# The last layer of a four-layer transformer kernel: routing moved into the decay stage, one expert put inside each pair of heads, the experts' sum kept in a buffer

## The chip, the cores and the metric

The kernel runs on one core of one Trainium2 chip. The time is the device time of one launch in microseconds, as the median of three runs. The engines are TensorE (PE; its weight loads are listed as PEld), VectorE (DVE), ScalarE (ACT), GpSimd (POOL) and SyncE (SP), which only issues transfers. Each executes its own list of instructions in order, and semaphores connect them.

## The reference

The input x has 2 batches of 1024 tokens, 256 wide (T = 2048 tokens). There are four layers. In each, x is normalised and an attention part and a feed-forward part, both fed with the same normalised xn, are added to x. Only the last layer is touched.

```python
xn = _layernorm(x, axis=-1)
x = x + _L3_attn_ref(xn, ...) + _L3_ffn_ref(xn, ...)

# attention part: 32 heads, P = N = 64
zxbca = xn @ W_in.T                       # split into x_t, z_t, b_t, c_t, a_log
decay = exp(-exp(a_log))                  # one number per token and head
states = states * decay + x_t b_t         # a scan over the tokens
y = (states . c_t + x_t * D) * silu(z_t)
y = layernorm(y) * gamma + beta ;  return y @ W_out.T

# feed-forward part: 32 experts, 32 further columns without an expert, K = 8
scores = softmax(xn @ w_cls.T) ;  topk_idx = top_k(scores + bias, 8)
w = scores[topk_idx] / sum * 1.5
buf[e, pos] = xn of the tokens of expert e, at most CAP = 128 of them
y = (silu(g) * u) @ w_down[e],  g, u = split(buf[e] @ w_gate_up[e])
out = sum over k of w * y, times (1 + sum of w without an expert)
```

Since both parts read xn and only xn, the feed-forward part doesn't depend on the attention part of its layer.

## The kernel before, in words

x is kept transposed in SBUF as XT (128 partitions by 2 by 2048), its normalised form as XN beside it. A layer is a sequence of stages. Each stage is a block in which every engine gets its list of instructions; between blocks all engines meet. Products of float32 accuracy for the projections are made of three fp32r products: an operand is split into a rounded part (hi) and the rest (lo), and `split_product` (L199) adds hi*hi, hi*lo and lo*hi, over two halves of the 256 rows, so six passes of 512 columns for each bank. Matmuls of float32 take two passes.

The last layer has these stages:

1. The norm, n3.
2. `l3_decays`: the decays of all heads (L1965 to L1989), stored to DRAM as running products and as themselves; the bias column bcol from beta (L1970), and the output weights wout scaled by gamma on DVE (L1995).
3. For each batch: `split_stage` of XN into XH and XL; `l3_pairs`; `l3_output`, which normalises Y, multiplies by wout and adds to XT (L2330).
4. `moe_route` (L2399 to L2523): the logits (L2428), the softmax and the top 8 on DVE, for each expert a running number of each of its tokens (`place`, L2439), the table of token numbers and weights `info`, and `key`. XN and XT are transposed to rows of tokens (L2436) and stored to DRAM: XN as moe_xtok, XT as the first content of the kernel's output.
5. `moe_experts`: for each of 32 experts a one-hot matrix of 128 slots by 2048 tokens (DVE, L2658), a product with `info` that gives the token number and weight of each slot (`mx_ptab`, L2609), the index (DVE, L2666 to L2672), a gather of 128 rows (POOL, L2587), two transposes (L2621), gate and up (L2628), silu (ACT, L2647), the product with up (DVE, L2684), down (L2635), the weight (ACT, L2650), and a scatter that adds the rows to the output in DRAM (POOL, L2597). Indices, gathered rows and weights are double-buffered or better.

`l3_pairs` runs over 16 pairs of heads, and in each over two halves z of the batch's tokens (512 each). The first pair is written out, the other 15 are a loop. The order in the half (h, z) is:

- TensorE: project x, b, c, z into four banks (L199), the outputs of the half before (L2097, L2102), the transposes of x (L2110) and b (L2114), the scores (L2121), the sums for the states pds (L2128), which need btok and xtok.
- ACT: copies xT, bT, cT; silu of z to sz; with z = 1 the hi part of the next pair's weights (L2145); xtok (L2167).
- DVE: two scans that build the decay table (L2221), cdT (L2224), the skip term of the half before (L2212, into the tile skip), btok (L2232), mixT (L2235), dsm (L2239), three or four updates of the state (L2246, L2250).
- POOL: with z = 1 the lo part of the next weights (L2189); for the half before, Y = skip * sz (L2179, "the gate") and ysum += Y (L2185).
- SP: the pair's weights (w4), the decays as table input (decb) and as rows (prow), and D (dcol).

The tiles xtok, mixT, sz, xT, cdT have two buffers, and the banks px, pb, pc, pz, pds, py one each; psc takes two.

Of the kernel before, what the change touches and what calls it, by code (L numbers as in the profile page):

```python
# [7 lines left out]
F32 = mybir.dt.float32  # L8
# [8 lines left out]
P = 128  # L17
# [146 lines left out]
def split_stage(nc, name, src, hi, lo):  # L164
# [4 lines left out]
    with Stage(nc, name) as st:  # L169
# [3 lines left out]
        with nc.Block() as block:  # L173
# [13 lines left out]
            @block.gpsimd  # L187
            def _(pool):
                for i, (c, tok) in enumerate(parts):
                    if i % 3 == 2:  # L190
                        pool.wait_ge(rounded, i + 1)
                        pool.tensor_tensor(lo[:, c, tok], src[:, c, tok], hi[:, c, tok].bitcast(F32), ALU.subtract)

# [1710 lines left out]
def l3_attn(nc, k, a):  # L1904

    decays = nc.dram_tensor("l3_decays", [2, L3_HEADS, T], F32, kind="Internal").ap()
    with Stage(nc, "l3w") as sw:
        wout = sw.sb("wout", [P, L3_PAIRS, D])  # L1910
        bcol = sw.sb("bcol", [P, DC])
        l3_decays(nc, k, a, decays, wout, bcol)
        for b in range(B):
            l3_batch(nc, k, a, decays, b, wout, bcol)


def l3_batch(nc, k, a, decays, b, wout, bcol):
    with Stage(nc, f"l3a{b}") as st:
        Y = st.sb("Y", [P, L3_PAIRS, S])
        ysum = st.sb("ysum", [P, S])  # L1920
        with Stage(nc, f"l3x{b}") as sx:
            XH, XL = sx.sb("XH", [P, DC, S], F32R), sx.sb("XL", [P, DC, S], F32R)
            split_stage(nc, f"l3s{b}", k.XN[:, :, b * S:(b + 1) * S], XH, XL)
            l3_pairs(nc, k, a, decays, b, Y, ysum, XH, XL)
# [5 lines left out]
def l3_decays(nc, k, a, decays, wout, bcol):  # L1930


    with Stage(nc, "l3d") as st:
# [6 lines left out]
        acc = [st.ps(f"acc{i}") for i in range(2)]  # L1940
        loaded, made, exped, decayed, prods, stored = st.sem("loaded"), st.sem("made"), st.sem("exped"), st.sem("decayed"), st.sem("prods"), st.sem("stored")
        zeroed = st.sem("zeroed")
        gb = st.sb("gb", [P, 2, L3_PAIRS])
        pbeta = st.ps("pbeta")
        w_loaded, beta_made = st.sem("w_loaded"), st.sem("beta_made")
        with nc.Block() as block:

            @block.sync
            def _(sp):
                sp.dma_start(w[:, :, :], rows(a["L3_wa"])).then_inc(loaded, 16)  # L1950
                sp.dma_start(gb[:, :, :], a["L3_gb"]).then_inc(w_loaded, 16)
                sp.dma_start(wout[:, :, :], rows(a["L3_W_outT"])).then_inc(w_loaded, 16)
                sp.wait_ge(prods, NCH)
# [3 lines left out]
                sp.wait_ge(stored, 32)  # L1957

            @block.tensor
            def _(pe):  # L1960
                pe.wait_ge(loaded, 16)
                for j in range(NJ):
                    wait(pe, exped, j - 1)
                    for c in range(DC):
                        mm = pe.matmul(acc[j % 2][0:H, :], w[:, c, :], k.XN[:, c, j * BANK:(j + 1) * BANK], start=(c == 0), stop=(c == DC - 1))  # L1965
                    mm.then_inc(made, 1)
# [4 lines left out]
                mm.then_inc(beta_made, 1)  # L1971

            @block.scalar
            def _(act):
                for j in range(NJ):
                    act.wait_ge(made, j + 1)
                    act.activation(ex[:, j % 2, :], acc[j % 2][0:H, :], ACT.Exp).then_inc(exped, 1)
                    act.wait_ge(exped, j + 1)
                    act.activation(dec[:, j * BANK:(j + 1) * BANK], ex[:, j % 2, :], ACT.Exp, scale=-1.0).then_inc(decayed, 1)

            @block.vector
            def _(dve):
                dve.memset(zero[:, :], 0.0).then_inc(zeroed, 1)
                dve.wait_ge(zeroed, 1)
# [7 lines left out]
                dve.wait_ge(beta_made, 1)  # L1992
                dve.tensor_copy(bcol[:, :], pbeta[:, 0:DC])
                for i in range(L3_PAIRS):
                    dve.tensor_scalar(wout[:, i, :], wout[:, i, :], gb[:, 0, i:i + 1], None, ALU.mult)  # L1995


def l3_pairs(nc, k, a, decays, b, Y, ysum, XH, XL):


    with Stage(nc, f"l3p{b}") as st:
# [11 lines left out]
        xtok = st.sb("xtok", [P, 2, QUAD, P])  # L2013
        btok = st.sb("btok", [P, QUAD, P])
        table = st.sb("table", [P, 2, BANK])
        mixT = st.sb("mixT", [P, 2, 2, BANK])
        dsm = st.sb("dsm", [P, QUAD, P])
        state = st.sb("state", [P, 2, QUAD, P])
        skip = st.sb("skip", [P, BANK])
# [790 lines left out]
```

## Time and profile before

| | us |
|---|---|
| median of three runs | 3949.11 (3946.87 to 3950.89) |
| span of the profiled execution | 3953.8 |
| PE busy in it | 3518.6 (89%) |
| DVE busy | 2363.0 (60%) |
| ACT busy | 1546.2 (39%) |
| POOL busy | 1385.1 (35%) |

The span goes from the first to the last instruction of the profiled execution, and it is the only time given for that execution; the median of the unprofiled runs is 4.7 us below it. A busy share is a mean over all stages. The page of the profile cuts the span in 40 slices of about 99 us; the last layer fills the last twelve of them.

### The profile page before, as it was taken

Reading aid. Unit: us, or ns where it says so; the run is one execution under the profiler, and the core shown is the slowest. Engines: PE = TensorE matmul, PEld = TensorE weight load, DVE = VectorE, ACT = ScalarE, POOL = GpSimd, SP = SyncE. Lnnn points to the kernel's source line nnn. Section 1 sums busy time; section 2 is a strip of 40 time slices with the busy share of each in tenths; the row PEclk is TensorE's granted clock in tenths of the full one; section 3 lists DMA queues with packets and bytes.
Section 4 is the critical chain, followed back from the end, with each engine's and each line's share of the span. In section 5 each row is a group of like instructions: output and inputs, shape, how many; then the busy total and the mean of one; then the engine's idle time right before and its main releaser. Section 6 shows DMA issues by size and latency. Waiting matters only on the chain. (4 is left out here: it accounts for less than half of the span.)

```text
span 3953.8 us, 65993 instructions
## 1 busy us (share of the span) xinstructions
PE 3518.6 (89%) x21608; PEld 2645.3 (67%) x21608; DVE 2363.0 (60%) x4783; ACT 1546.2 (39%) x2820; POOL 1385.1 (35%) x1085
## 2 busy tenths in 40 slices
PE   6899999999796999999995779998699988999576
PEld 4777777777574888888872445554388847886354
DVE  3555555655423566666654879885477756776454
ACT  2444444444333444444432236664333333333121
POOL 1333333332133666666652200000133352335144
PEclk8999999999898999999997879999799998999755
DMA  0000000000001000000000412221233304331144
GB/s 33 7 5 3 5 5 3 5 5 5 33 0 43 13 18 17 17 17 17 17 5 22 171 65 82 80 83 39 65 93 103 105 10 107 98 96 48 60 108 96
DMA packets 115990, 178.66 MB, mean 45 GB/s; under 512 B 22288, under 2 KB 65040, under 8 KB 115600
## 3 DMA queue, kind: packets, MB, share of 16 engines
q1 hardware_dynamic: 109776, 169.38, 13.7%
q0 software_dynamic: 6144, 8.39, 1.3%
q8 instruction: 38, 0.62, 0.1%
q14 instruction: 32, 0.26, 0.0%
HBM read 151.51 MB, written 25.95 MB: 45 GB/s over the span
## 5 line engine op out<-in xcount | busy, mean ns | idle before, releaser
L424 POOL TENSOR_TENSOR l0h_probs<-l0h_probs,l0h_inv 128x128 f32<-128x128 f32 (+7 forms) x256 | 292.7, 1146 | 585.4 <-DVE l0h_inv L459 585.4
L1775 DVE TENSOR_REDUCE l2h_half<-l2h_s 128x1 f32<-128x512 f32 x512 | 337.3, 685 | 48.0 <-PE l2h_s L1677 47.0
L355 PE MATMUL l0h_sc<-l0a_KT,l0h_QT 128*128 x768 | 296.7, 499 | 29.8 <-ACT l0h_probs L528 28.3
L1762 ACT ACTIVATE l2h_PT<-l2h_s 128x1024 f32<-128x1024 f32 x256 | 248.3, 1022 | 162.6 <-PE l2h_s L1687 162.5
L382 PE MATMUL l0h_cx<-l0h_PT,l0h_VG 128*128 128x128 f32 x2304 | 300.7, 276 | 0.0
L528 ACT ACTIVATE l0h_probs<-l0h_sc,l0h_negtop 128x128 f32<-128x128 f32 (+7 forms) x256 | 189.6, 741 | 245.0 <-DVE l0h_negtop L454 244.6
L382 PEld LDWEIGHTS l0h_cx<-l0h_PT,l0h_VG 128*128 128x128 f32 x2304 | 278.0, 192 | 1.1
L159 POOL TENSOR_TENSOR XN<-XN,n_rstd 128x512 f32<-128x512 f32 x32 | 39.8, 1266 | 595.8 <-DVE n_rstd L140 595.8
L1677 PE MATMUL l2h_s<-l2h_K,l2h_Q 128*128 128x512 f32 x512 | 218.5, 466 | 23.2 <-DMA l2h_K<-l_split 21.0
L452 DVE TENSOR_REDUCE l0h_top<-l0h_sc 128x1 f32<-128x128 f32 (+7 forms) x256 | 193.9, 758 | 8.8
L355 PEld LDWEIGHTS l0h_sc<-l0a_KT,l0h_QT 128*128 128x128 f32 x768 | 125.7, 192 | 106.3 <-issue 63.6
L391 PE MATMUL l0h_outp<-l0h_ctxT,l0h_wd 128*128 128x128 f32 x1024 | 163.8, 283 | 24.8 <-ACT l0h_ctxT L521 11.7
L369 PEld LDWEIGHTS l0h_tp<-ident,l0h_probs 128*128 128x128 f32 x1152 | 138.6, 141 | 64.1 <-issue 39.5
L1677 PEld LDWEIGHTS l2h_s<-l2h_K,l2h_Q 128*128 128x128 f32 x512 | 99.2, 195 | 113.4 <-DVE l2h_half L1775 74.7
L369 PE MATMUL l0h_tp<-ident,l0h_probs 128*128 128x128 f32 x1152 | 168.7, 273 | 0.0
L470 DVE COPY l0h_PT<-l0h_tp 128x256 f32<-128x256 f32 (+2 forms) x192 | 98.6, 514 | 114.2 <-PE l0h_tp L369 112.4
L2189 POOL TENSOR_TENSOR l3p_w_lo<-l3p_w,l3p_w_hi 128x1024 fp32r<-128x1024 f32 x34 | 80.1, 2356 | 241.1 <-ACT l3p_w_hi L2145 241.1
L391 PEld LDWEIGHTS l0h_outp<-l0h_ctxT,l0h_wd 128*128 128x128 f32 x1024 | 134.2, 191 | 44.7 <-ACT l0h_ctxT L521 31.2
L514 ACT ACTIVATE l0h_PT<-l0h_tp 128x512 f32<-128x512 f32 (+1 forms) x192 | 100.8, 525 | 159.8 <-PE l0h_tp L369 159.3
L2221 DVE TENSOR_TENSOR_SCAN l3p_table<-l3p_decb,l3p_eye 128x512 f32<-128x512 f32 x128 | 149.6, 1210 | 22.8 <-DMA l3p_blk<-c_l_block 17.3
L1687 PE MATMUL l2h_s<-l2h_Q,l2h_K 128*128 128x512 f32 x512 | 161.7, 399 | 0.0
L2179 POOL TENSOR_TENSOR l3a_Y<-l3p_skip,l3p_sz 128x512 f32 (+1 forms) x64 | 81.6, 1276 | 208.9 <-DVE l3p_skip L2212 208.9
(408 smaller groups left out, 8954.9 us busy)
## 6 DMA issues: line engine op xcount, KB each, us to landing
l3p_decb<-l_decays SPq DMA_DIRECT2D x128, 256.0 KB, 4.2
l3p_w<-L_w SPq DMA_DIRECT2D x34, 512.0 KB, 3.7
l2h_Q<-l_split SPq DMA_DIRECT2D x64, 256.0 KB
l2h_K<-l_split SPq DMA_DIRECT2D x64, 256.0 KB
l3p_prow<-l_decays SPq DMA_DIRECT2D x128, 128.0 KB, 2.9
l_split<-l2q_hi SPq DMA_DIRECT2D x16, 512.0 KB, 4.1
l_split<-l2q_lo SPq DMA_DIRECT2D x16, 512.0 KB, 3.8
mx_wgu<-L_ffn_w_gate_up SPq DMA_DIRECT2D x32, 256.0 KB
```

What stands on the lines that cost most here:

```text
L355: mm = pe.matmul(sc[u % 2][:, lo:lo + n], QT[:, u * P:(u + 1) * P], KT[:, ds(g, 1), b * S + lo:b * S + lo + n], start=True, stop=True)
L369: mm = pe.transpose(tp[n % 2][:, (kb - q) * P:(kb - q + 1) * P], probs[:, u % 4, kb * P:(kb + 1) * P], k.ident[:, :])
L382: mm = pe.matmul(cx[:, 0:P], VG[:, b * NQ + kb, :], PT[:, u % 2, kb, :], start=(kb == 0), stop=(kb == t))
L391: mm = pe.matmul(outp[:, c * P:(c + 1) * P], wd[:, c * P:(c + 1) * P], ctxT[:, u % 2, :], start=True, stop=True)
L424: pool.tensor_tensor(p, p, inv[:, u % 4:u % 4 + 1].to_broadcast([P, keys(u)]), ALU.mult).then_inc(probs_scaled, 1)
L452: dve.reduce_max(top[:, u % 2:u % 2 + 1], sc[u % 2][:, 0:keys(u)], AX_X).then_inc(top_ready, 1)
L528: act.activation(probs[:, u % 4, 0:keys(u)], sc[u % 2][:, 0:keys(u)], ACT.Exp, bias=negtop[:, u % 2:u % 2 + 1], scale=L0_SCALE, accum_out= ...
L1677: pe.matmul(bank(slot_of(i))[:, :], Q1[:, b, t * P:(t + 1) * P], K1[:, b, z * BANK:(z + 1) * BANK], start=True, stop=True).then_inc(s1_mad ...
L1687: mm = pe.matmul(s2[kb % 2][:, z * BANK:(z + 1) * BANK], K2[:, b, kb * P:(kb + 1) * P], Q2[:, b, z * BANK:(z + 1) * BANK], start=True, sto ...
L1762: act.activation(PT[:, b, kb, :], s2[kb % 2][:, :], ACT.Exp, scale=L2_SCALE).then_inc(exped, 1)
L1775: dve.reduce_max(half[:, b, t, z:z + 1], bank(slot_of(i))[:, :], AX_X).then_inc(s1_read, 1)
L2221: dve.tensor_tensor_scan(table[:, i, :], decb[:, o, i, :], eye4[:, :], 0.0, ALU.mult, ALU.add).then_inc(tables, 1)
```

## The change

Layer 3 becomes one function, `l3_layer`, with these stages:

- `l3_front` takes the place of `l3_decays` and `moe_route`. It holds the decays, the routing, the table, and the rows of XN. The rows of XT and their store to the output are gone. A zeroed tile is stored to a new DRAM buffer, moe_acc. The scaling of wout and the copy of bcol are ACT's.
- `split_in_place`: only XH has a tile of its own. XL is written over XN, through a second name (XNL) for the same memory. All its subtractions are DVE's.
- `l3_pairs` carries expert 16 b + h inside pair h of batch b. The loop is now over pairs 1 to 14; pairs 0 and 15 are written out.
- `l3_finish` loads moe_acc, transposes XT to rows, adds, and stores the output in four parts and a last row of tiles.

Two PSUM banks were needed: pds now shares the bank of pz, and the freed bank pm holds gathered rows or the down product in its left half, table or gate and up in its right one. To make room in SBUF, xtok and mixT have one buffer, and skip is gone: DVE writes to Y and POOL multiplies Y in place. The experts' tiles have one buffer each.

The core of the diff, the front:

```diff
+def l3_front(nc, k, a, decays, wout, bcol, moe):
             @block.sync
-                sp.dma_start(w[:, :, :], rows(a["L3_wa"])).then_inc(loaded, 16)
+                sp.dma_start(w[:, :, :], rows(a["L3_wa"])).then_inc(wa_loaded, 16)
+                sp.dma_start(wcls[:, :, :], rows(a["L3_ffn_w_clsT"])).then_inc(loaded, 16)
...
+                sp.wait_ge(zero_rows, 2)
+                sp.dma_start(rows(acc), rowsZ[:, :, :]).then_inc(stored, 16)
...
+                sp.wait_ge(tr_act, turns)
+                sp.dma_start(rows(xtok), rowsN[:, :, :]).then_inc(stored, 16)
             @block.tensor
...  (decay products as before)
+                pe.wait_ge(loaded, 80)
+                for t in range(TT):
+                    for c in range(DC):
+                        mm = pe.matmul(lg[:, t * MOE_N:(t + 1) * MOE_N], k.XN[:, c, t * P:(t + 1) * P], wcls[:, c, :], ...)
+                mm.then_inc(logits_made, 1)
+                for n in range(turns):   # the transposes of XN
...
                 pe.wait_ge(w_loaded, 32)   # pbeta
...
+                pe.wait_ge(counted, 1)     # place
             @block.vector
...  (decay scans as before, then the routing of moe_route, unchanged)
```

Inside the pairs, TensorE and DVE:

```diff
                 def step(h, z):
-                    project(h, z)
+                    project(h, z, (0, 1))
+                    if z == NZ - 1:
+                        gate_up(h)
+                    project(h, z, (2, 3))
                     if not is_first(h, z):
                         outputs(*before(h, z))
-                    tables_and_states(h, z)
+                    if z == 0:
+                        turn_rows(h)
+                    else:
+                        down(h)
+                    scores(h, z)
+                    if z == NZ - 1 and more(h):
+                        table(h + 1)
+                    state_sums(h, z)      # now also waits for z_kept
+                table(0)
                 steps(pe, step)
@@ DVE, in step(h, z), after cdT
+                    if z == NZ - 1:
+                        gate_expert(h)
+                    if more(h):
+                        mark(h + 1, z)    # one half of the one-hot
                     if not is_first(h, z):
                         add_skip(*before(h, z))
@@ after mixT, which now waits for y_made of the half before
+                    if z == 0:
+                        keep_index(h)
+                    elif more(h):
+                        make_index(h + 1)
                     dve.wait_ge(ds_made, n + 1)
@@ ahead of the steps
+                dve.wait_ge(e_consts, 32)
+                mark(0, 0)
+                mark(0, 1)
+                make_index(0)
+                def keep_index(e):
+                    dve.wait_ge(indexed, e + 1)
+                    wait(dve, scattered, 16 * e)
+                    dve.tensor_copy(index_out[:, :], index_in[:, :]).then_inc(kept_index, 1)
+                    wait(dve, weighed, e)
+                    dve.tensor_copy(wcol[:, :], idw[:, 1:2]).then_inc(kept_index, 1)
```

POOL, ACT and SP:

```diff
@@ POOL
                 def step(h, z):
                     if z == NZ - 1:
                         split_weights(h + 1)
+                        if more(h):
+                            gather(h + 1)
                     if not is_first(h, z):
                         gate(*before(h, z))
+                    if z == NZ - 1:
+                        scatter(h)
@@ ACT, z == 1: after cT
+                        act.activation(gated[:, :], pm[:, D:D + P], ACT.Silu).then_inc(sg_kept, 1)
@@ ACT, z == 1: after the split of the next weights
+                        act.wait_ge(down_made, h + 1)
+                        act.wait_ge(kept_index, 2 * h + 2)
+                        wait(act, scattered, 16 * h)
+                        act.activation(ye[:, :], pm[:, XR], ACT.Copy, scale=wcol[:, 0:1]).then_inc(weighed, 1)
@@ ACT, z == 0: after xtok
+                        act.activation(xgT[:, :], pm[:, XR], ACT.Copy).then_inc(xg_kept, 1)
@@ SP, in load(h, z), between decb and prow
+                    if z == NZ - 1:
+                        wait(sp, gu_made, h)
+                        sp.dma_start(wgu[:, :, :], a["L3_ffn_w_gate_up"][ds(E0 + h, 1)]...).then_inc(e_loaded, 16)
+                        wait(sp, down_made, h)
+                        sp.dma_start(wdn[:, :], a["L3_ffn_w_down"][ds(E0 + h, 1)]...).then_inc(e_loaded, 16)
@@ SP, ahead of load(0, 0)
+                sp.dma_start(slots[:, :], a["c_moe_slots"].to_broadcast([P, P])).then_inc(e_consts, 16)
+                sp.dma_start(spare[:, :], a["c_moe_spare"]).then_inc(e_consts, 16)
```

The last stage:

```diff
+def l3_finish(nc, k, a, acc):
+                sp.dma_start(summed[:, :, :], rows(acc)).then_inc(loaded, 16)
+                for i in range(PARTS):      # 4
+                    t = slice(i * TT // PARTS, (i + 1) * TT // PARTS)
+                    sp.wait_ge(added, (i + 1) * N // PARTS)      # N = 8
+                    sp.dma_start(rows(a["out"])[:, t, :], out_rows[:, t, :]).then_inc(stored, 16)
...
+                for n in range(N):          # TensorE
+                    wait(pe, added, n - 3)
+                    ... four transposes of XT into tr[n % 4]
+                for n in range(N):          # DVE
+                    dve.wait_ge(turned, n + 1)
+                    dve.tensor_tensor(out_rows[:, t, :], summed[:, t, :], tr[n % 4][:, :]..., ALU.add).then_inc(added, 1)
```

## Rows read from the trace of the kernel before

**Rows 1.** Busy time by stretch, with granted clock (PEclk), DMA share and GB/s.

```profile
3539.97:3560.96 20.99, 20.99 (x161) 17.88 (x160) 15.56 (x22) 6.92 (x11) 7.45 (x6) 1.00 0.35 100
...
3745.00:3950.00 205.00, 141.56 (x896) 102.23 (x896) 97.44 (x160) 37.34 (x97) 96.47 (x64) 0.50 0.45 102
```

**Rows 2.** Timeline, stage borders: start us, us, engine, line, operation, idle and releaser.

```profile
3690.51 0.75 DVE L2330 SCALAR_TENSOR_TENSOR XT<-l3o_tmp,l3w_bcol,XT 128x512 f32<-128x512 f32 x1
...
3692.22 0.40 SPq L2405 DMA_DIRECT2D mr_wcls<-L_ffn_w_clsT  x1
...
3740.95 0.69 DVE L2523 SCALAR_TENSOR_TENSOR moe_key<-mr_maskE,mr_place 128x512 f32<-128x512 f32 x1
...
3943.78 1.57 POOL L2597 DMA_INDIRECT out<-mx_y,mx_index  x1 [4.42 <-ACT mx_y L2650]
```

**Rows 3.** DMA issues (KB, us to landing), and transposes in the timeline.

```profile
l3w_wout<-L_W_outT SPq DMA_DIRECT2D x1, 2048.0 KB, 8.5
...
out<-mr_rowsX SPq DMA_DIRECT2D x1, 2176.0 KB, 10.6
...
3712.10 3.62 PE L2436 MATMUL mr_tr<-ident,XN 128*128 128x128 f32 x16
```

**Rows 4.** DMA issues of POOL in the experts: count, us to landing.

```profile
mx_xg<-moe_xtok,mx_index POOLq DMA_INDIRECT x32, 2.7
...
out<-mx_y,mx_index POOLq DMA_INDIRECT x32, 4.0
```

**Rows 5.** Decays and logits: busy time in two windows, then the timeline.

```profile
2822.00:2826.00 4.00, 4.00 (x30) 3.62 (x28) 2.79 (x9) 1.24 (x3) 0.00 (x0) 0.87 0.00 0
...
3698.00:3712.00 14.00, 13.61 (x64) 13.61 (x65) 1.62 (x2) 0.00 (x0) 0.00 (x0) 0.50 0.00 1
...
2822.39 11.51 PE L1970 MATMUL l3d_pbeta<-l3d_gb,l3w_wout 128*128 128x1 f32 x64
...
2834.01 4.28 DVE L1995 TENSOR_SCALAR l3w_wout<-l3w_wout,l3d_gb 128x256 f32<-128x256 f32 x16
...
3698.39 13.91 PE L2428 MATMUL mr_lg<-mr_wcls,XN 128*128 128x64 f32 x64 [14.14 <-DMA mr_again<-c_moe_again]
...
3712.34 1.23 DVE L2463 TENSOR_REDUCE mr_small<-mr_lg 128x16 f32<-128x1024 f32 x1 [10.85 <-PE mr_lg L2428]
```

**Rows 6.** Timeline of single experts: TensorE, DVE.

```profile
3758.97 0.61 PE L2609 MATMUL mx_ptab<-moe_info,mx_onehot 128*128 128x7 bf16 x16
...
3759.87 1.22 PE L2635 MATMUL mx_py<-mx_wdn,mx_gated 128*128 128x256 f32 x2 [0.28 <-DVE mx_gated L2684]
...
3912.65 0.17 DVE L2666 TENSOR_REDUCE mx_idw<-mx_ptab 128x2 f32<-128x6 f32 x1
...
3913.10 0.16 DVE L2672 TENSOR_TENSOR mx_index<-mx_spill,mx_idw 128x1 uint32<-128x1 f32 x1
...
3913.25 2.29 DVE L2658 TENSOR_TENSOR mx_onehot<-mx_slots,moe_key 128x2048 bf16<-128x2048 f32 x1
```

**Rows 7.** Timeline: first instructions of the pairs, and one half (z = 0).

```profile
2849.59 0.80 PE L199 MATMUL l3p_px<-l3x_XH,l3p_w_hi 128*128 128x512 f32 x1 [15.70 <-POOL l3p_w_lo L2189]
...
2850.76 2.34 DVE L2221 TENSOR_TENSOR_SCAN l3p_table<-l3p_decb,l3p_eye 128x512 f32<-128x512 f32 x2 [8.56 <-DMA l3p_blk<-c_l_block]
...
3550.37 0.47 PE L199 MATMUL l3p_px<-l3x_XH,l3p_w_hi 128*128 128x512 f32 x1
...
3560.05 1.16 PE L2128 MATMUL l3p_pds<-l3p_xtok,l3p_btok 128*128 128x128 f32 x8
```

**Rows 8.** Timeline of DVE and POOL in the same pair.

```profile
3541.29 1.12 DVE L2250 SCALAR_TENSOR_TENSOR l3p_state<-l3p_state,l3p_prow,l3p_dsm 128x128 f32<-128x128 f32 x3
...
3551.18 1.29 POOL L2185 TENSOR_TENSOR l3a_ysum<-l3a_ysum,l3a_Y 128x512 f32<-128x512 f32 x1 [0.21 <-POOL l3a_Y L2179]
...
3551.43 1.97 DVE L2250 SCALAR_TENSOR_TENSOR l3p_state<-l3p_state,l3p_prow,l3p_dsm 128x128 f32<-128x128 f32 x3
...
3559.12 0.69 DVE L2232 TENSOR_TENSOR l3p_btok<-l3p_pb,l3p_table 128x512 f32<-128x512 f32 x1 [0.23 <-PE l3p_pb L2114]
```

More of the change, by code:

```diff
@@ L1927, in l3_batch @@
         clear_semaphores(nc)
-def l3_decays(nc, k, a, decays, wout, bcol):
-    with Stage(nc, "l3d") as st:
+def l3_front(nc, k, a, decays, wout, bcol, moe):
+    key, info, xtok, acc = moe.key, moe.info, moe.xtok, moe.acc
+    with Stage(nc, "l3f") as st:
         H = L3_HEADS
@@ L1991, in _, with per_tile @@
                 dve.memset(dec[:, :].rearrange("h (i n) -> h i n", n=P)[:, :, 0:1], 0.0).then_inc(zeroed, 1)
[L1992 to L1998, printed above, removed]
+                def per_tile(i):
+                    return small[:, i, :].unsqueeze(2).to_broadcast([P, TT, MOE_N])
@@ L2001, in l3_pairs @@
+def l3_pairs(nc, k, a, decays, b, Y, ysum, XH, XL, moe):
+    E0 = b * L3_PAIRS
+    key, info, xrows, acc = moe.key, moe.info, moe.xtok, moe.acc
     with Stage(nc, f"l3p{b}") as st:
@@ L2033, in steps, with more @@
                 step(0, z)
-            with engine.Fori(1, L3_PAIRS) as h:
+            with engine.Fori(1, L3_PAIRS - 1) as h:
                 for z in range(NZ):
                     step(h, z)
+            for z in range(NZ):
+                step(L3_PAIRS - 1, z)
+        def more(h):
+            return not isinstance(h, int) or h + 1 < L3_PAIRS
         def before(h, z):
@@ L2129, in tables_and_states, with table, turn_rows @@
                     mm.then_inc(ds_made, 1)
+                def table(e):
+                    pe.wait_ge(marked, 2 * e + 2)
+                    wait(pe, weighed, e)
+                    for t in range(TT):
+                        mm = pe.matmul(pm[:, TAB], onehot[:, t, :], info[:, ds(E0 + e, 1), t, :].rearrange("p a n -> p (a n)"), start=(t == 0), stop=(t == TT - 1))
+                    mm.then_inc(tabled, 1)
+                def turn_rows(e):
+                    pe.wait_ge(gathered, 16 * e + 16)
+                    pe.wait_ge(indexed, e + 1)
+                    for c in range(DC):
+                        mm = pe.transpose(pm[:, c * P:(c + 1) * P], xg[:, c * P:(c + 1) * P], k.ident[:, :])
+                    mm.then_inc(g_turned, 1)
@@ L2731 @@
 SPLIT_LAYERS = (0, 1)
[L2732 removed]
+LAYERS = [(l0_attn, l0_ffn), (l1_attn, l1_ffn), (l2_attn, l2_ffn)]
 def program(nc, a):
```

583 lines of the change are left out of this document (269 added, 314 removed).

## The prediction

> **What bounds the kernel now.** I read the busy shares by stage first. Within one pair of heads TensorE is busy for the whole of its 20.99 us at full clock, DVE 74%, ACT 33%, POOL 35%; in the experts it is busy 69% at half clock and waits in between [rows 1]. So the pairs are TensorE's, and whatever is put into them costs its TensorE time and no more, as long as nothing it waits for is late. The experts are a chain of short steps and transfers with nobody saturated. The timeline gives the stage borders: the attention's last instruction ends at 3691.3 us (3690.51 + 0.75), the routing's last at 3741.6, and the last scatter is issued at 3943.8 in a span of 3953.8 [rows 2]. Routing and experts together hold 3953.8 - 3691.3 = 262.5 us at the end, which the change dissolves.
>
> **1. What is removed, and the last stage.** 262.5 us go. In their place: 1.0 us to enter a stage (3691.3 to the routing's first load at 3692.2), the load of acc, the additions, the stores. A 2,048 KB load took 8.5 us to landing, the 2,176 KB store to out 10.6 [rows 3]. Four transposes take 0.9 us at half clock [rows 3]; the first four groups lie under the load, the others are chained to the additions (0.7 us each), so the last addition ends about 5.2 us behind the landing. The stores start 1.6 us behind it and need 10.6, which ends later. Behind a landing comes what the old end shows: 10.0 us from the issue of the last scatter to the end of the span, less its 4.0 us to landing [rows 2, 4], so 6.0. Sum: 1.0 + 8.5 + 1.6 + 10.6 + 6.0 = 27.7; as the chain by the additions gives only 25, I take 27 (bounds 22 and 34). Net: **-235.5**.
>
> **2. The front stage.** The order written for TensorE puts the logits behind the decay products, so the routing starts only at 2822.4 [rows 5], and its five loads, issued behind one other on SP's queue, have landed by then: at the old place the logits could start 6.2 us behind the first of them (3698.4 against 3692.2), which here is 2817.5 [rows 2, 5]. The logits took 13.9 us, all at half clock; DVE's chain from their end (3712.3) to the key (3741.6) is 29.3 us [rows 5]. Now the logits follow matmuls that ended at full clock: the mean of 2822 to 2826 is 0.87, so some 3 us more at full clock [rows 5]. Those halve: I take 11.0 us (bounds 7.0, all fast, and 13.9). The stage ends at 2822.4 + 11.0 + 29.3 = 2862.7 instead of 2838.3 (2834.01 + 4.28) [rows 5]: **+24.5** (20.5 to 27.5). Under this chain at no cost: transposes of XN, pbeta (11.5 us on TensorE, over at about 2853), the product for place, the zeros and both large stores (POOL and the DMA engines are idle), and the scaling of wout, which moves to ACT (16 from about 2853 on; ACT's mean in a pair, 6.92 us for 11 mostly twice as wide [rows 1], puts their end at 2863 at the latest). That cover is the thinnest: what ACT takes beyond it lengthens the stage one for one.
>
> **3. The start of the pairs, twice.** TensorE began at 2849.6, DVE at 2850.8, when its constants had landed [rows 7]. Now two more DMAs stand ahead of them on SP (+0.8), DVE makes both halves of the one-hot (2.29 us for a whole one [rows 6]) and TensorE's queue begins with table(0) (0.6), which waits for them. 1.2 + 0.8 + 2.4 + 0.6 = 5.0, twice: **+10** (8 to 13). The splitting's fourth subtraction goes from POOL to DVE; ACT's rounding sets its end as before: 0.
>
> **4. Inside the pairs, 32 times: TensorE.** A pair takes 20.99 us [rows 1]. Added are 8 passes of gate and up; eight such 128x128 passes took 0.91 us in the pairs (3560.05 to the border at 3560.96) [rows 1, 7]. The down product: 1.22 us for two passes at half clock, 0.43 at full without its tail; two transposes 0.25 (sixteen took 3.62 at half clock [rows 3]); 16 table products 0.61 at half clock, of which a floor of issue may stay: 0.4 [rows 6]. Sum **2.0** (1.8 to 2.3, with a bubble at each of four waits).
>
> **5. Inside the pairs: who may be late.** Per pair DVE gets 2 x 1.2 (mark), 0.3, 0.6 (index, from the reduction to the last of three) and 0.3, so 3.6 on its 15.6 of now 23; ACT 1.1; POOL 1.0 to 2.4 for a gather and 1.6 for a scatter [rows 6, 4]. None is full. I follow one pair, time 0 being the start of its second half (z = 1) at TensorE. Gate and up stand at 2.9, DVE's product for them is done at 7.2, down stands at 8.1: hidden. ACT's w_hi still ends before 8.2, POOL's w_lo by 10.8, the next pair starts at 12.0. The table is at 10.8 to 11.2; DVE makes the index behind mixT, by 12.8, so 0.8 into the next pair. POOL's gather is queued there, ahead of the gate of the first half: issued at 1.0, landed at 3.8 (2.7 to landing [rows 4]), wanted by turn_rows at 7.6: 3.8 us spare. SP's two weight loads wait for the previous expert's products; behind them stands prow, which waits longer, for the states at 3.4 of the next pair, so they hold back nothing. The scatter goes out near 6 and lands near 10; DVE's keep_index asks for it at 11, and what is queued behind that (dsm, the states) has over 3 us until TensorE's outputs.
>
> The narrow place is btok. In the first half it ended 0.24 us before TensorE's product of it started (3559.12 + 0.69 against 3560.05, 9.7 us into the pair) [rows 7, 8]. The transposes of the gathered rows give 0.25 more, and make_index pushes DVE's dsm back by 0.4, which the wait for y_made absorbs only if mark (1.2) is over by then. And the gate on POOL, held back by the gather, now falls beside DVE's state updates and scans. A row shows what that costs: three updates took 1.12 us alone, but 1.97 where POOL's ysum of 1.29 began 0.25 before them [rows 8].
>
> The Trainium skill (SBUF — State Buffer, Who interferes with whom) states it as a rule: a Vector instruction with two SBUF inputs and a GpSimd instruction that reads SBUF exclude each other, the first to start keeping the port for its whole length. By that rule the scans and mark, too, stand back behind POOL, which no row here shows for them; by rule alone the time would be that of rival B.
>
> Without a collision btok ends at 9.7, wanted at 9.9: stall 0. If POOL's first pass stands in a scan's way and the second in mark's way, I get btok at 10.25 and the product at 10.5: stall 0.6. If both passes precede a scan each: 1.3. I take **0.6**, a pair then costs 2.6, and 32 x 2.6 = **+83** (58 at 1.8 and no stall, 144 at 4.5, if scatter and gather should each hold DVE for another microsecond).
>
> **Sum.** -235.5 + 24.5 + 10 + 83.2 = -117.8: the span of 3953.8 becomes 3836.0. The median of the runs, 3949.1, is 4.7 under the profiled span; I keep that distance: **3831 us**.
>
> **Rivals.** A, no collision: DVE keeps its slack and a pair costs TensorE's 2.0 alone: 19 us less, **3812**. For it: its 23 us hold only 19 of DVE; against: POOL's gate now starts just where the states run. B, both POOL passes get ahead: 3.3 per pair, 22 more, **3854**. For it: the 1.97 row; against: the scans are issued back to back, so POOL has to win a tie.
> C, slower than before: the gathered rows come late. turn_rows stands in TensorE's in-order queue ahead of the scores of both heads, so each microsecond of delay past the 3.8 spare is one of stall, 32 times. It decides from 118 / 32 = 3.7 us of stall, when a gather takes 2.8 + 3.8 + 3.7 = 10.3 us from issue to landing. If it took 12, the stall is 5.4 and the time 3831 + 173 = **4004**, and a lower granted clock after such gaps would come on top. For it: gather and scatter share POOL's one queue with the gate, and decay rows are read at a DMA share of 0.35; against: with the experts' share of 0.45 it landed in 2.7 [rows 1, 4].
> D, the change does only half of what it says: the front is serial, the decays hiding nothing. That is already in the 24.5.
> [...]
>
> **How the numbers follow.** Forecast 0.45 (own range 3818 to 3845), A 0.2, B 0.2, C 0.05; 0.1 remains for a front, start or end outside its bounds by tens of microseconds. The range takes in A and B with their bounds, 3798 to 3880. All but C and a part of the last are faster by over 0.2% (8 us, what this kernel's measurement can tell from nothing): faster 0.92, same 0.02, slower 0.06.
>
> **What would show it.** Right: a pair of 23 to 24 us, TensorE still full and at full clock there; a front stage of 52 us, its logits partly fast; 27 us behind the attention; first projection 5 us later than before in each batch. The stall of step 5 would be an idle of 0.3 to 1.3 us ahead of the product of btok in first halves alone, with POOL's gate over a scan. Wrong: TensorE waiting for the gather or for DVE's product of the expert, a granted clock under 0.95 in the pairs, or DVE busy through a whole pair.

## The result, and the profile after

The changed kernel takes 3836.7 us (median of four runs, 3834.8 to 3841.9) against 3949.2 us before on the same chip: a ratio of 0.971 (95% interval 0.970 to 0.972). The profiled execution has a span of 3840.0 us against 3953.8, 113.8 less; 117.8 less was predicted. By stage, from the timelines of both:

| part | before, us | after, us | difference | predicted |
|---|---|---|---|---|
| ahead of the front | 2810.8 | 2811.4 | +0.5 | 0 |
| front, to VectorE's last result | 27.5 | 48.3 | +20.9 | +24.5 |
| start of the pairs, both batches | 24.2 | 33.8 | +9.7 | +10 |
| pairs, to the output stage, both | 693.8 | 790.8 | +96.9 | +83.2 |
| output stages, both | 135.0 | 136.4 | +1.4 | 0 |
| behind the last output stage | 262.5 | 19.4 | -243.1 | -235.5 |

The front in the timeline of after (start, duration, engine, line, operation, operands; in brackets the idle time before and what ended it):

```profile
2811.35 0.37 SPq L2008 DMA_DIRECT2D l3f_w<-L_wa  x1
2822.92 7.36 PE L2042 MATMUL l3f_lg<-l3f_wcls,XN 128*128 128x64 f32 x64
2830.32 1.22 DVE L2099 TENSOR_REDUCE l3f_small<-l3f_lg 128x16 f32<-128x1024 f32 x1 [3.47 <-PE l3f_lg L2042]
2858.98 0.69 DVE L2159 SCALAR_TENSOR_TENSOR l3w_key<-l3f_maskE,l3f_place 128x512 f32<-128x512 f32 x1
```

The logits start at 2822.9, 0.5 us behind the 2822.4 of the prediction, and take 7.36 us where they took 13.9 [rows 5]. VectorE's chain behind them, from 2830.32 to 2859.67, is 29.3 us as read before. ScalarE's scaling of wout ended at 2856.5, inside it, so the thin cover held.

The start of the first batch of pairs:

```profile
2863.37 0.37 SPq L2259 DMA_DIRECT2D l3p_slots<-c_moe_slots  x1
2867.53 0.43 SPq L2263 DMA_DIRECT2D l3p_blk<-c_l_block  x1
2869.78 2.34 POOL L2443 TENSOR_TENSOR l3p_w_lo<-l3p_w,l3p_w_hi 128x1024 fp32r<-128x1024 f32 x1 [5.45 <-ACT l3p_w_hi L2386]
2873.48 2.36 DVE L2491 TENSOR_TENSOR l3p_onehot<-l3p_slots,l3w_key 128x1024 bf16<-128x1024 f32 x2 [10.37 <-DMA l3p_blk<-c_l_block]
2875.90 0.59 PE L2338 MATMUL l3p_pm<-l3w_info,l3p_onehot 128*128 128x7 bf16 x16 [22.65 <-DVE l3p_onehot L2491]
2876.34 0.77 PE L222 MATMUL l3p_px<-l3x_XH,l3p_w_hi 128*128 128x512 f32 x1
```

The weights are split at 2872.1, and nothing else that the first projection reads comes later. In TensorE's order it stands behind the table, which needs the marks (the one-hot), and these stand behind VectorE's wait for blk, a constant they don't use.

One pair, from the first projection product of its second half (z = 1) to that of the next pair's:

```profile
3656.18 0.48 PE L222 MATMUL l3p_px<-l3x_XH,l3p_w_hi 128*128 128x512 f32 x1
3659.02 1.05 PE L2353 MATMUL l3p_pm<-l3p_xgT,l3p_wgu 128*128 128x128 f32 x8
3664.47 0.70 PE L2359 MATMUL l3p_pm<-l3p_wdn,l3p_gated 128*128 128x256 f32 x2
3667.06 1.36 PE L2338 MATMUL l3p_pm<-l3w_info,l3p_onehot 128*128 x16
3669.26 0.48 PE L222 MATMUL l3p_px<-l3x_XH,l3p_w_hi 128*128 128x512 f32 x1
3680.29 0.48 PE L222 MATMUL l3p_px<-l3x_XH,l3p_w_hi 128*128 128x512 f32 x1
```

A window over exactly this stretch, with busy time and count of each engine, then the granted clock, the DMA share and GB/s:

```profile
3656.18:3680.29 24.11, 23.99 (x190) 20.41 (x188) 20.59 (x30) 7.73 (x14) 11.05 (x7) 1.00 0.50 114
```

The half z = 1 takes 13.08 us (10.40 before), the half z = 0 10.92 in the first batch and 11.03 in the second (10.6 before). TensorE (first number after the length) is busy for all but 0.1 us, at full clock. The table products (L2338) are the row out of line: 1.36 us for 16 products which took 0.59 at the start of the batch, shown above, and 0.61 at half clock before [rows 6]. From 3667.06 the next work of TensorE follows 1.31 us later.

Where the predicted collision would be (z = 0, VectorE and GpSimd):

```profile
3597.80 0.99 POOL L2449 DMA_INDIRECT l3p_xg<-moe_xtok,l3p_index_in  x1 [3.26 <-DVE l3p_index_in L2505]
3597.95 3.82 DVE L2567 SCALAR_TENSOR_TENSOR l3p_state<-l3p_state,l3p_prow,l3p_dsm 128x128 f32<-128x128 f32 x3
3598.82 1.30 POOL L2434 TENSOR_TENSOR l3a_Y<-l3a_Y,l3p_sz 128x512 f32 x1
3600.33 1.29 POOL L2439 TENSOR_TENSOR l3a_ysum<-l3a_ysum,l3a_Y 128x512 f32<-128x512 f32 x1 [0.20 <-POOL l3a_Y L2434]
3601.69 2.33 DVE L2529 TENSOR_TENSOR_SCAN l3p_table<-l3p_decb,l3p_eye 128x512 f32<-128x512 f32 x2
3601.78 2.54 POOL L2456 DMA_INDIRECT moe_acc<-l3p_ye,l3p_index_out  x1 [0.16 <-issue]
```

Three state products take 3.82 us, against 1.12 and 1.97 in [rows 8]. The scans behind them start when GpSimd's second pass has just ended, and keep their 1.17 us each.

The end of a batch of pairs, in the kernel before (first line) and after, and the last stage of after:

```profile
3196.47 0.17 DVE L2314 MEMSET l3o_avg<- 128x128 f32 x1 [3.21 <-PEq L2044]
...
3264.57 0.75 DVE L2485 SCALAR_TENSOR_TENSOR l3a_Y<-l3p_xT,l3p_dcol,l3p_py 128x512 f32<-128x512 f32 x1 [3.19 <-PE l3p_py L2302]
3266.86 1.26 POOL L2439 TENSOR_TENSOR l3a_ysum<-l3a_ysum,l3a_Y 128x512 f32<-128x512 f32 x1 [0.20 <-POOL l3a_Y L2434]
3271.17 0.17 DVE L2631 MEMSET l3o_avg<- 128x128 f32 x1 [5.85 <-PEq L2236]
...
3820.92 0.38 SPq L2690 DMA_DIRECT2D fin_summed<-moe_acc  x1
3829.57 4.29 DVE L2714 TENSOR_TENSOR fin_out_rows<-fin_summed,fin_tr 128x512 f32<-128x512 f32 x7 [8.93 <-DMA fin_summed<-moe_acc]
3830.88 4.23 SPq L2694 DMA_DIRECT2D out<-fin_out_rows  x4
3835.16 0.81 SPq L2695 DMA_DIRECT2D out<-fin_summed  x1
```

The idle time ahead of the output stage is 5.85 us; before it was 3.21. The last stage is a chain of load (8.6 us), eight additions (5.2) and a last store: 19.4 us.

### The profile page after: what moved, and what is told of

It is laid out like the page before. It is cut to its first block and busy times, and to the rows that moved or that the text cites. A ratio compares the mean times of both kernels' runs of the same rounds, so it can differ in the third digit from the quotient of the medians.

```text
span 3840.0 us, 66211 instructions
## 1 busy us (share of the span) xinstructions
PE 3466.9 (90%) x21608; PEld 2618.4 (68%) x21608; DVE 2420.7 (63%) x4872; ACT 1537.1 (40%) x2827; POOL 1403.2 (37%) x1083
## 5 line engine op out<-in xcount | busy, mean ns | idle before, releaser
L378 PE MATMUL l0h_sc<-l0a_KT,l0h_QT 128*128 x768 | 298.2, 501 | 29.2 <-ACT l0h_probs L551 27.5
L414 PE MATMUL l0h_outp<-l0h_ctxT,l0h_wd 128*128 128x128 f32 x1024 | 163.9, 283 | 24.5 <-ACT l0h_ctxT L544 11.7
L994 ACT ACTIVATE l1a_kswap<-l1a_pk,l1a_bias 64x512 f32<-64x512 f32 x64 | 43.8, 685 | 278.3 <-PE l1a_pk L222 278.3
```

The lines of the kernel that those rows point to most:

```text
L378: mm = pe.matmul(sc[u % 2][:, lo:lo + n], QT[:, u * P:(u + 1) * P], KT[:, ds(g, 1), b * S + lo:b * S + lo + n], start=True, stop=True)
L414: mm = pe.matmul(outp[:, c * P:(c + 1) * P], wd[:, c * P:(c + 1) * P], ctxT[:, u % 2, :], start=True, stop=True)
```

## The experiments

Each names what it changes in the kernel after. Their ratios are to the kernel before on the same chip.

### The table at a fixed expert

```diff
-  pe.matmul(pm[:, TAB], onehot[:, t, :], info[:, ds(E0 + e, 1), t, :]..., start=(t == 0), stop=(t == TT - 1))
+  pe.matmul(pm[:, TAB], onehot[:, t, :], info[:, E0:E0 + 1, t, :]..., start=(t == 0), stop=(t == TT - 1))
```

> The 16 table products of every pair read the token table at a fixed expert instead of at the loop's expert, so the experts' gate weights belong to the wrong expert (each row still gets one); all else is as in the changed kernel. Theory 1: the table costs 1.31 us in the loop's pairs against 0.42 to 0.56 in the written-out ones because each product's address comes from a loop register. Then the table falls to 0.4 to 0.6 us in every pair, the pair from 24.0 to about 23.1 us, and 28 or so loop pairs take 23 to 27 us off: about 3812 us (ratio to before 0.965). Rival: the table is slow because of what the other engines do to its operands beside it (or because its operand was written shortly before): then it stays at 1.3 us, the pair at 24.0 and the time at 3836.

Measured: 3818.5 us, ratio 0.967 (0.965 to 0.969). The 16 products of 12 pairs (2905 to 3200 us) grouped by line, in the kernel after and then here (count | busy us, mean ns | idle before):

```profile
L2338 PE MATMUL l3p_pm<-l3w_info,l3p_onehot 128*128 x192 | 16.2, 173 | 0.0
```

```profile
L2338 PE MATMUL l3p_pm<-l3w_info,l3p_onehot 128*128 128x7 bf16 x192 | 6.7, 167 | 0.0
```

Per pair that is 1.35 us and then 0.56. The mean of one hardly moves (173 and 167 ns): a product isn't slower, they follow each other at 82 ns on average instead of 26. The trace's records, register instructions included, have the reason: in the loop each of the 16 has one more instruction on TensorE's queue, which makes the operand's address from the loop's register, 448 of them in 28 loop pairs; in the written-out pairs and in this kernel there is none. With them the first eight products of a table start about 26 ns apart and the others 124; without them all do at about 26. The half z = 1 falls from 13.09 to 12.20 us. The gain, 18 us, is smaller than the expected 23 to 27 because z = 0 grew from 10.92 to 11.15 (11.03 to 11.26 in the second batch), which the next experiment shows as well.

The register address alone doesn't fix the price. The experts' loop of the kernel before had it too (384 such instructions for 24 experts), and there a table took 0.72 us on average (0.61 to 1.15), because 12 to 16 of its products started about 27 ns apart before the first gap of 124. The written-out experts took 0.59 to 0.61. Why more products come close together there was not tested.

### The expert's slice of the table, copied

```diff
+  def keep_info(e):
+      wait(act, tabled, e)
+      act.activation(einfo[:, :], info[:, ds(E0 + e, 1), :, :]..., ACT.Copy).then_inc(info_kept, 1)
@@ ACT, z == 0: after xgT:  keep_info(h + 1)
@@ PE, table(e):
+  pe.wait_ge(info_kept, e + 1)
-  ... info[:, ds(E0 + e, 1), t, :] ...
+  ... einfo[:, t * MOE_INFO:(t + 1) * MOE_INFO] ...
```

> ScalarE copies the expert's slice of the token table into a tile at a fixed address, once per pair in the half after xgT, and the table products read that tile; the full computation. Theory 1 (loop-register addresses): table 0.4 to 0.6 us, pair about 23.1, time 3810 to 3816 if ScalarE's copy (0.3 to 0.5 us more per pair, it is busy 40%) stays beside TensorE. Rival 1 (the table is slow for another reason): 3836. Rival 2 (the added copy delays ScalarE's xT copies, on which the scores wait): the pair loses up to 0.5 us in the half z = 0, so that 8 to 15 of the 25 us come back.

Measured: 3817.6 us, 0.967 (0.965 to 0.969); halves of 12.20 and 11.15 (11.26). The address theory stands with the whole computation in place: one register-addressed instruction on ScalarE instead of 16 on TensorE. Rival 2 has the right half, z = 0, which lost 0.23 us per pair, but the wrong reason. What z = 0 lost is TensorE's wait for btok, in all products of btok of 13 pairs:

```profile
L2333 PE MATMUL l3p_pz<-l3p_xtok,l3p_btok 128*128 128x128 f32 x208 | 29.8, 286 | 2.9 <-DVE l3p_btok L2554 2.9
```

2.9 / 13 = 0.22 us per pair by this row; by the halves it is 0.30 and 0.40, against the 10.85 us of the next experiment, where the wait is 0. The fixed-expert kernel, which has no copy on ScalarE, has the same 2.9, and in the kernel after this row read 1.1. One pair shows how GpSimd's two passes now fall:

```profile
3577.62 2.70 DVE L2577 SCALAR_TENSOR_TENSOR l3p_state<-l3p_state,l3p_prow,l3p_dsm 128x128 f32<-128x128 f32 x3
3580.25 3.37 DVE L2539 TENSOR_TENSOR_SCAN l3p_table<-l3p_decb,l3p_eye 128x512 f32<-128x512 f32 x2
3580.37 2.16 POOL L2449 TENSOR_TENSOR l3a_ysum<-l3a_ysum,l3a_Y 128x512 f32<-128x512 f32 x1 [0.20 <-POOL l3a_Y L2444]
```

The second pass began 0.12 us behind the first scan and took 2.16 us instead of 1.29; the second scan, behind that pass, took 2.24 instead of 1.21. So the scans are held here, in 30 of the 32 pairs, which in the kernel after happened in 2.

### The gating product ahead of the gather

```diff
@@ POOL, step(h, z)
   split_weights(h + 1)
-  if more(h): gather(h + 1)
   gate(*before(h, z))
+  if more(h): gather(h + 1)
   scatter(h)
```

> GpSimd does the gating product of the pair ahead of the gather instead of behind it; the full computation. The collision that the prediction priced at 0.6 us per pair was seen at 3.83 us for three state products on VectorE beside gather and gate, with the wait of the gather's turn-over at TensorE for the token column at 0.05 to 0.3 us. Theory: the stall in z = 0 is that collision; with the gate first the state products run 1.5 to 2.5 us and the 0.05 to 0.3 us of stall go, 2 to 8 us in all: 3829 to 3835. Rival: the gather, 1.3 us later, lands too late for its turn-over and its wait grows: the pair gets longer than 24.0 and the time is 3840 or more. Rival 2: the extra 0.05 in z = 0 isn't a stall by the collision: no change, 3836.

Measured: 3831.9 us (3831.7 to 3838.0), 0.971 (0.969 to 0.972), 4.8 less than after. The runs of both kernels overlap (3834.8 to 3841.9 there), so what follows rests on the halves in the traces. Timeline of z = 0, then the row of btok:

```profile
3592.73 1.27 POOL L2439 TENSOR_TENSOR l3a_ysum<-l3a_ysum,l3a_Y 128x512 f32<-128x512 f32 x1 [0.20 <-POOL l3a_Y L2434]
3594.67 1.13 DVE L2567 SCALAR_TENSOR_TENSOR l3p_state<-l3p_state,l3p_prow,l3p_dsm 128x128 f32<-128x128 f32 x3
3594.89 1.01 POOL L2449 DMA_INDIRECT l3p_xg<-moe_xtok,l3p_index_in  x1 [0.89 <-DVE l3p_index_in L2505]
...
L2331 PE MATMUL l3p_pz<-l3p_xtok,l3p_btok 128*128 128x128 f32 x200 | 28.6, 286 | 0.0
```

The states are back at 1.13 us although the gather's issue lies right beside them, so the two passes of the gate held them, not the gather. z = 0 becomes 10.85 us in both batches: the stall was 0.07 per pair in the first and 0.18 in the second, 30 x 0.12 = 3.8 us. The transposes of the gathered rows (the turn-over) aren't waited for, so the first rival falls. The slack shows too: between the states and btok VectorE now waits four times, 0.19, 0.46, 0.89 and 0.42 us, and in the kernel after not at all.

### No experts in the pairs

All expert work is out of the pairs (marks, index, table, gather, products, scatter and the loads of their weights), and the output lacks that layer's experts.

> The experts are taken out of the pairs: no marks, index, table, gather, turn-over, gate/up, down, scatter and no loads of their weights there (the output lacks the experts' contribution of this layer); the front and the finish stay. Theory: all of the pair's growth (20.99 to 24.0) is the expert's own TensorE work and stalls, and the pair falls back to 20.99 exactly, the gap between the last pair and the output stage from 5.9 back to 3.2 us of VectorE idle time and the start of a batch by about 5 us: 32 x 3.0 + 2 x 2.6 + 2 x 5 = 111 us less than 3836, about 3725. Rival: part of the growth is from the rearrangement (weight splits, gating and queue order around the experts' places): then the pair stays above 21.2 us and the time above 3732. Rival on the end gap: if it is not the last scatter's, it stays at 5.9 us.

Measured: 3733.4 us, 0.946 (0.944 to 0.947). From the first projection product of a batch to that of its last half are 326.3 and 327.2 us here, 326.2 and 325.9 before and 370.7 and 371.8 after: of the growth of 90.4, 1.4 is left without experts, so next to nothing is from the rearrangement. A pair before is 21.05 us on this measure. The start and the end of a batch:

```profile
2867.61 2.34 POOL L2416 TENSOR_TENSOR l3p_w_lo<-l3p_w,l3p_w_hi 128x1024 fp32r<-128x1024 f32 x1 [5.48 <-ACT l3p_w_hi L2372]
2870.00 0.80 PE L222 MATMUL l3p_px<-l3x_XH,l3p_w_hi 128*128 128x512 f32 x1 [18.70 <-POOL l3p_w_lo L2416]
...
3215.96 0.17 DVE L2587 MEMSET l3o_avg<- 128x128 f32 x1 [3.21 <-PEq L2236]
```

The projection starts with the split's end, and the end gap is 3.21 us: both went with the experts. The whole gain, 103 us, is 8 short of the 111 expected. By the traces (104.4 in all) the pairs with their end gaps gave 96.4 where 101 was taken (3.0 for each of 32 pairs, but the last halves hold no table), and the two starts 8.0 where 10 was.

### The marks ahead of the wait for the constants

```diff
@@ DVE
-  dve.wait_ge(consts, 32)
   mark(0, 0); mark(0, 1); make_index(0)
+  dve.wait_ge(consts, 32)
```

> VectorE's wait for the two constants of the scans (eye4 and blk) moves behind the first two marks and the first index; the full computation. Theory: what makes a batch of pairs start late is that the first marks stand behind a wait for constants they don't use (blk landed at 2873.48 while the weights' split, which the first projection waits for, ended at 2872.12): the marks run from about 2867, the table comes before the split's end and the first projection at 2872.1 instead of 2876.3, 4.2 us per batch, 8 in all: about 3828. Rival: the marks wait for the slots' load as long as for blk (it is the tail of DMA landing that counts): under 2 us per batch, time 3834 or more.

Measured: 3828.9 us, 0.970 (0.968 to 0.971), 7.7 less than after, as expected; in the traces the two starts of the pairs take 25.6 us together instead of 33.8.

```profile
2864.82 0.37 SPq L2259 DMA_DIRECT2D l3p_slots<-c_moe_slots  x1
2868.76 2.36 DVE L2489 TENSOR_TENSOR l3p_onehot<-l3p_slots,l3w_key 128x1024 bf16<-128x1024 f32 x2 [4.20 <-DMA l3p_spare<-c_moe_spare]
2871.18 0.59 PE L2338 MATMUL l3p_pm<-l3w_info,l3p_onehot 128*128 128x7 bf16 x16 [16.56 <-DVE l3p_onehot L2489]
2873.54 0.79 PE L222 MATMUL l3p_px<-l3x_XH,l3p_w_hi 128*128 128x512 f32 x1 [1.77 <-POOL l3p_w_lo L2443]
```

From the first load to the projection are 8.7 us instead of 13.0, and what the projection waits for is the split of its weights again.

### The product with beta ahead of the logits

```diff
@@ PE, l3 front
+  pe.wait_ge(w_loaded, 32);  64 products of wout with gb into pbeta
   pe.wait_ge(loaded, 80);    64 products of XN with wcls into lg
   the transposes of XN
-  pe.wait_ge(w_loaded, 32);  64 products of wout with gb into pbeta
```

> In the front the 64 one-column products of wout with beta go ahead of the 64 router products instead of behind them; the full computation. The logits were seen at 7.36 us right behind the decays' products at full clock, where the prediction took 11.0 and the kernel before showed 13.91 at the low clock. Theory 1 (the clock decides what the logits cost, and one-column work for 10 us lets it fall): pbeta takes 6.5 to 10.8 us, then the logits 11 to 13.9 instead of 7.36; the routing chain starts 12 to 17 us later and the front is as much longer: 3849 to 3854. Rival (the clock doesn't fall over pbeta, or the logits' time isn't the clock's): the logits stay at 7.4 us and the front grows by pbeta's 6.5 to 10.8 alone, less 0.2: 3843 to 3847.

Measured: 3862.7 us, 0.978 (0.976 to 0.979): 26 more than after, which neither theory had.

```profile
2826.37 13.81 PE L2042 MATMUL l3f_pbeta<-l3f_gb,l3w_wout 128*128 128x1 f32 x64 [2.15 <-DMA l3w_wout<-L_W_outT]
2840.04 13.89 PE L2047 MATMUL l3f_lg<-l3f_wcls,XN 128*128 128x64 f32 x64
```

```profile
2834.00:2846.00 12.00, 12.00 (x57) 12.00 (x58) 0.00 (x0) 0.00 (x0) 0.00 (x0) 0.50 0.00 0
```

The logits take 13.89 us at a granted clock of 0.50 (1.2 GHz), as at their old place, and 7.36 at 1.00 (2.4 GHz) right behind the decays' 512-column products. These are the same 64 products, so theory 1 holds in that the clock decides what the logits cost. What let it fall isn't separated: TensorE first waited 2.15 us for wout, the clock was 1.00 until 2826, a mean of 0.66 in the microsecond from there and 0.50 from 2827 on, so it fell as the one-column work began and not over it. (A wait alone didn't do it in the kernel after: 3.27 us ahead of L2049 were at 1.00, and the clock fell about 1.4 us into the transposes behind it.) Theory 1's sum was short since the beta products, taken at 6.5 to 10.8, ran at half clock as well (13.8 us) and first waited for wout. Being busy for 12 us on end didn't bring the clock back. The Trainium skill (TensorE: Matmul & The Clock Gate, Part 1) has the throttled state as the default and sustained activity as what releases it. The 0.50 of this window fits the first half; on the second the measurement decides: here, as in [rows 5], being busy without a gap didn't release it.

### Who waits for the last scatter, and no last scatter

```diff
@@ POOL, end of the pairs
-  pool.wait_ge(scattered, 16 * L3_PAIRS)
@@ SP, end of the pairs
+  sp.wait_ge(scattered, 16 * L3_PAIRS)
```

> At the end of a batch of pairs SyncE instead of GpSimd waits for the last scatter; the full computation. Without experts in the pairs the gap between VectorE's last operation and the output stage fell from 5.85 to 3.21 us. Theory 1: it is GpSimd's queue that needs 2.6 us at the end of a stage in which it issued transfers of its own, wherever the wait stands: the gap stays at 5.85 us and the time at 3836. Rival 1: it is GpSimd's wait for the scatter itself: the gap goes to 3.2 us, twice 2.6 us: 3831. Rival 2: the scatter's landing holds the stage back whoever waits: it stays too, but then the landing, at about 3264.4, would have to be later than the last gating product at 3268.1, which the trace speaks against.

Measured: 3836.6 us, 0.972 (0.970 to 0.973), no change. (One of the five executions, the profiled one, took 10340 us and is not read; the gap with this edit is read in the last kernel below.)

The other leaves the last pair's scatter out of each batch, and with it that expert's contribution:

> The scatter of each batch's last pair is left out, and the wait for it, so the output lacks that expert's contribution; the 15 scatters and 16 gathers before it stay. With SyncE's wait in place of GpSimd's the gap at the end of the pairs stayed at 5.85 us, against 3.21 without experts. Theory 1 (GpSimd ends a stage 2.6 us later once it has issued transfers in it, whichever): the gap stays at 5.85. Rival (it is the last scatter, issued 8 us before the stage's end, that GpSimd still works off): the gap falls to 3.2 us, and twice 2.6 us go: one time near 3831.

```profile
3259.80 1.26 POOL L2439 TENSOR_TENSOR l3a_ysum<-l3a_ysum,l3a_Y 128x512 f32<-128x512 f32 x1 [0.20 <-POOL l3a_Y L2434]
3263.93 0.95 POOL L2623 MEMSET l3o_sqsum<- 128x1024 f32 x1 [2.87 <-POOLq L2236]
3264.03 0.17 DVE L2631 MEMSET l3o_avg<- 128x128 f32 x1 [5.77 <-PEq L2236]
```

One run, 3834.4 us. The gap stays at 5.77 us though GpSimd's last transfer was issued 26 us before its last pass: neither the wait nor the last scatter makes it. The trace's records, waiting instructions included, show where the time is. Each block ends with a drain on GpSimd, and all other engines are released behind it: it ends 2.7 us behind GpSimd's last pass in the kernel after, 2.6 in this one and 0.1 in the kernel without experts, whose GpSimd lacks the gathers, the scatters and the wait for them, and nothing else. So it is GpSimd, once it has issued transfers in the stage. Whether one would do as well as 31 was not tried.

### All mends together

The copy, the gate first, the marks first and SyncE's wait as above, and the projection's weights loaded ahead of slots and spare:

```diff
@@ SP
-  slots, spare;  load(0, 0)
+  load(0, 0) with slots and spare issued right behind its w4
```

> All mends together, the full computation: ScalarE's copy of the token table for the expert, the gating product ahead of the gather, the marks ahead of the wait for eye4 and blk, the projection's weights loaded ahead of the slots and the spare rows at the start, SyncE's wait for the last scatter. If the three mechanisms are apart from each other the pair is 12.20 + 10.85 = 23.05 us instead of 24.06 (32 us in all, 30 with the written-out pairs left out), each batch starts 4.2 to 5 us earlier, and the end gap gives 0 to 5: 3837 - 30 - 9 = 3798, or 3793 with the gap. Rival: the mends overlap, since the shorter pair brings the gather and the marks closer (the token-column stall was 0.22 us per pair with the copy alone): the z = 0 half stays at 11.1 to 11.25 us and the time is 3803 to 3808.

Measured: 3799.3 us (five runs, 3796.9 to 3822.2), 0.964 (0.962 to 0.966): 37 us, 1.0%, less than the kernel after by the medians, and the fastest that computes everything. By the ratios it is 0.7%, since two of the five runs took 3807.0 and 3822.2.

```profile
2862.98 4.50 DVE L2500 TENSOR_TENSOR l3p_onehot<-l3p_slots,l3w_key 128x1024 bf16<-128x1024 f32 x2 [4.50 <-DMA l3p_spare<-c_moe_spare]
2863.63 2.77 POOL L2455 TENSOR_TENSOR l3p_w_lo<-l3p_w,l3p_w_hi 128x1024 fp32r<-128x1024 f32 x1 [3.93 <-ACT l3p_w_hi L2391]
2867.99 0.77 PE L222 MATMUL l3p_px<-l3x_XH,l3p_w_hi 128*128 128x512 f32 x1
...
3247.02 0.17 DVE L2641 MEMSET l3o_avg<- 128x128 f32 x1 [5.85 <-PEq L2238]
```

The halves are 12.16 and 10.85: inside the pairs the mends add up, and the rival (they overlap) falls. The start shows one new cost: the marks take 4.50 us instead of 2.36 beside GpSimd's subtraction, which they now meet. The two starts take 27.0 us together where the marks ahead of the wait alone gave 25.6, so no gain from loading the weights first is to be seen. The last row is the end gap with SyncE's wait, still 5.85.

## Why the prediction was right, and where its terms were off

The structure was right: 262.5 us of low-clock routing and experts went, the pairs stayed TensorE's at full clock, and the expert cost them its TensorE time. The sum was 4.0 us out in the span (3840.0 against 3836.0) and 6 in the median. That it came so close is luck: the pairs cost 13.7 us more than forecast, the last stage 7.6 and the front 3.6 less.

- **Last stage** (-235.5, measured -243.1). The load was right (8.6 to 8.5). The tail of 6.0 behind the last landing was taken from the old end; here it is about 1 (3840.0 less the last store's issue at 3835.2 and its 3.7 to landing). The old end was that of a block in which GpSimd had issued 64 transfers, and its drain there took 5.3 us (from 3947.7), so the 6.0 was mostly the same cost that the end gaps show; in the new last stage GpSimd issues none. And the stores go out in parts under the additions, so 19.4 us instead of 27, below the lower bound of 22.
- **Front** (+24.5, measured +20.9). The one mis-sized term is the logits, 7.36 us where 11.0 was taken; the mean clock of 0.87 over four mixed microseconds was read as a clock about to fall, and it stayed at 1.00. The lower bound of 7.0 was the right one. That it is the clock at this place is shown by the beta experiment.
- **Start of the pairs** (+10, measured +9.7). Size right, and the step named the wait: the first marks behind the constants. It cost 4.2 us per batch that nothing requires, shown by moving the wait.
- **Pairs, TensorE** (2.0 per pair). Gate and up 0.91 as taken, down 0.53 for 0.43, turn-over 0.21 (10.85 less the 10.64 without experts) for 0.25. The table was the step that failed: 0.4 taken, "a floor of issue may stay", 1.31 measured, 0.88 of it the register addresses. The row it was sized from has the same 16 products, but at a fixed place; no bound of that term held it, and 28 loop pairs paid 25 us. The trace of before had 24 tables with register addresses, but they took 0.72 on average: they would have pointed at the cost and not given its size.
- **Pairs, stall** (0.6 per pair, measured 0.07 and 0.18). The place was right (btok in z = 0), and so was the mechanism (the gate beside the states); the collision itself, 2.7 us on VectorE, was even larger than either row said. Most of it fell into slack, the 2.0 us of waits that VectorE has between the states and btok in the gate-first kernel, of which the prediction counted 0.2 (btok at 9.7, wanted at 9.9). Once TensorE's own time shrank, the second scan was held as well and the stall rose to 0.3 to 0.4. The sign that the prediction named, GpSimd's gate over a scan, came only there (in the kernel after, in 2 of the 32 pairs). Rival A (no collision) has nearly the right stall for a wrong reason; B is excluded, and so is C: no wait for the gathered rows appears.
- **End of the pairs** (0, measured 2 x 2.6). Not foreseen: no term stood for the block's end, though the old end of the program, read for the last stage, held it.

On the rule the prediction weighed, the Trainium skill (SBUF — State Buffer, Who interferes with whom), the states agree: 3.82 us beside GpSimd's two passes, 1.13 without them. So do the marks, 4.50 beside a subtraction on GpSimd and 2.36 without, and the scans: 2.24 us with a pass of GpSimd's ahead of them in the copy kernel, 1.21 without, and the pass itself 2.16 behind a scan instead of 1.29. Beside the issue of a scatter they kept 1.17 us.

The added 96.9 us of the pairs are then: 28 x 0.88 = 25 for the addresses, 64 for the expert's own products (32 x 1.44 for gate, up and down, 30 x 0.43 for the tables, 32 x 0.21 for the turn-over, less 30 x 0.06, by which the half z = 1 at a fixed expert, 12.22, is shorter than its terms 10.41 + 0.91 + 0.53 + 0.43), 3.8 for the collision and 5.3 for the end gaps, 98 in all. Neither the 0.06 nor the 1 us too much is explained by a run.

## What to carry to other kernels

Size a short product inside a loop from a row whose operand moves with the loop, and don't trust the size even then: the same 16 products with register addresses took 0.72 us in one stage and 1.31 in another. Here they paid more for their addresses than for themselves, and one copy to a fixed tile on an engine with time to spare bought most of that back. When work is inserted into a stream bound by one engine, look for what it drags along at the borders: a wait for constants that stands ahead of the new first step, and the end of a block on the engine that now issues transfers. And where the clock is full, put the products that somebody waits for first: the same logits took 7.36 us right behind the long products and 13.89 behind a wait and 64 one-column products.

## What the runs showed of the hardware that was not expected

- Sixteen 7-column bf16 products with operands at a register's address take 1.31 us inside the pairs, at a constant address 0.43 (from the halves' difference of 0.88): the first eight start about 26 ns apart, the others 124. In the experts' loop before, 12 to 16 of them started close together, and the table took 0.72 us on average.
- A gather's issue on GpSimd beside three two-input products on VectorE costs them nothing (1.13 us); two tensor passes on GpSimd, of 2.6 us in all, hold them by 2.7. A scan behind such a pass took 2.24 us instead of 1.21, and a pass behind a scan 2.16 instead of 1.29.
- A block in which GpSimd issued transfers ended 2.6 us later, in GpSimd's drain at its end, whichever engine waited for the transfers and even with the last one issued 26 us before GpSimd's last pass.
- The same 64 products of 64 columns took 7.36 us behind wide products and 13.89 behind a wait of 2.15 us and one-column products, and 12 us without a gap at 0.50 didn't raise the clock.
